# A cross-attention layer in one queue order: hundreds of single steps of a hand-placed schedule moved

## The reference

```python
q = hidden_state @ Wq + bq            # 512 x 1024, 32 heads
k = encoder_hidden_state @ Wk + bk    # 512 x 256, 8 heads
v = encoder_hidden_state @ Wv + bv
scores = jnp.einsum('bkgld,bksd->bkgls', q, k) * scale + mask
attn = jax.nn.softmax(scores, axis=-1)
out = jnp.einsum('bkgls,bksd->bkgld', attn, v)
out = out.transpose(0, 3, 1, 2, 4).reshape(b, l, H) @ Wo + bo
x = out + hidden_state
return (x - mu) * jax.lax.rsqrt(var + EPS) * gamma + beta
```

## Time and profile before

| | us |
|---|---|
| median of 3 runs | 1751.57 |
| lowest and highest | 1750.95, 1754.67 |
| the profiled execution | 1751.32 |
| its span | 1749.3 |
| TensorE matmuls busy | 1602.6 (92%) |
| VectorE busy | 1448.7 (83%) |
| ScalarE busy | 1385.7 (79%) |
| GpSimd busy | 935.7 (53%) |

### The profile page before, as it was taken

One profiled execution on the slowest core, in us unless ns is written; L12 is line 12 of the kernel. 1 busy time (PEld: TensorE's weight loads), 2 busy tenths in 40 slices (PEclk: granted clock), 3 DMA queues, 4 the chain that ended last, 5 costly groups with the idle time before them and its releaser, 6 DMA issues. The chain is left out here.

```text
span 1749.3 us, 38438 instructions
## 1 busy us (share of the span) xinstructions
PE 1602.6 (92%) x14048; PEld 1110.0 (63%) x14048; DVE 1448.7 (83%) x2773; ACT 1385.7 (79%) x3186; POOL 935.7 (53%) x731
## 2 busy tenths in 40 slices
PE   3898879999899989999899998999989999999986
PEld 2665556576566765676576775667666676667654
DVE  4489878789788996889888898789988899788886
ACT  3578868769888787978889789787888878887794
POOL 5426433526754458534675448662585545856382
PEclk8999999999999999999999999999999999999998
DMA  9669987646885578664796567965678646875331
GB/s 178 186 148 227 241 232 199 182 135 168 250 257 144 138 187 286 188 154 122 209 288 185 130 175 192 287 178 127 174 238 252 158 133 170 292 208 150 84 114 67
DMA packets 357292, 325.02 MB, mean 186 GB/s; under 512 B 145776, under 2 KB 248176, under 8 KB 357104
## 3 DMA queue, kind: packets, MB, share of 16 engines
q1 hardware_dynamic: 357104, 322.56, 67.5%
HBM read 244.85 MB, written 83.89 MB: 188 GB/s over the span
## 5 line engine op out<-in xcount | busy, mean ns | idle before, releaser
L1941 PE MATMUL bank<-ring_hi,w_sb 128*128 128x512 f32 x2368 | 785.5, 399 | 32.1 <-issue 19.2
L1725 ACT ACTIVATE probs<-probs,shift 128x512 f32<-128x512 f32 x1024 | 726.9, 713 | 92.1 <-DVE shift L1826 91.0
L1839 DVE STREAM_TRANSPOSE turned_p<-probs 128x2048 f32<-128x2048 f32 x256 | 585.7, 2297 | 154.3 <-PE bank L2021 149.3
L1826 DVE CUSTOM_DVE_ANT_0 probs<-bank,mask_l 128x512 f32<-128x512 f32 x1024 | 643.1, 680 | 56.3 <-PE bank L2001 37.2
L1626 POOL TENSOR_TENSOR w_sb<-w_raw,w_sb 128x512 fp32r<-128x512 f32 x320 | 412.1, 1297 | 413.8 <-ACT w_sb L1682 413.7
L1941 PEld LDWEIGHTS bank<-ring_hi,w_sb 128*128 128x128 f32 x2368 | 444.4, 189 | 149.9 <-issue 42.6
L1941 PE MATMUL bank<-ring_lo,w_sb 128*128 128x512 f32 x1184 | 467.9, 395 | 0.0
L2001 PE MATMUL bank<-k_stack,q_stack 96*128 96x512 f32 x1024 | 358.9, 414 | 12.7 <-DVE shift L1826 10.0
L2021 PE MATMUL bank<-turned_p,v_all 32*32 32x512 f32 x8192 | 307.9, 642 | 65.8 <-DVE turned_p L1839 48.6
L1638 POOL TENSOR_TENSOR ring_lo<-x_t,ring_hi 128x512 fp32r<-128x512 f32 x168 | 214.7, 1291 | 144.9 <-ACT ring_hi L1694 144.4
L2001 PEld LDWEIGHTS bank<-k_stack,q_stack 96*128 96x128 f32 x1024 | 186.1, 189 | 143.3 <-issue 62.9
(11 more groups left out here) (75 smaller groups left out, 933.2 us busy)
## 6 DMA issues: line engine op xcount, KB each, us to landing
w_raw<-w_d SPq DMA_DIRECT2D x144, 256.0 KB, 3.7
q_stack<-q_hi_d SPq DMA_DIRECT2D x128, 256.0 KB, 4.3
w_raw<-in_L_xattn_Wo_dram SPq DMA_DIRECT2D x128, 256.0 KB, 3.0
q_hi_d<-part_hi SPq DMA_DIRECT2D x64, 256.0 KB, 3.9
q_lo_d<-part SPq DMA_DIRECT2D x64, 256.0 KB, 5.0
q_stack<-q_lo_d SPq DMA_DIRECT2D x64, 256.0 KB, 3.9
v_all<-v_d SPq DMA_DIRECT2D x256, 64.0 KB, 2.2
out_dram<-y_sb SPq DMA_DIRECT2D x32, 512.0 KB, 3.0
```

The lines of the kernel that those rows point to most:

```text
L1725: nc.scalar.activation(probs[:, st % 2, h, :], probs[:, st % 2, h, :], ACT.Exp, scale=-1.0, bias=shift[:, g % 2, i:i + 1], accum_out=sums[ ...
L1826: nc.vector.tensor_tensor_reduce(out=probs[:, st % 2, h, :], in0=S_ps[h][:, :], in1=mask_l[:, st, :], scale=-1.0, scalar=HIGHEST, op0=ALU. ...
L1839: nc.vector.transpose(turned_p[:, :, :, st, :].rearrange("p j h c -> p h j c"), probs[:, st % 2, :, :].rearrange("p h (j c) -> p h j c", c ...
L1941: mm = nc.tensor.matmul(C[c][:, :], w_sb[:, n_w, (1, 0, 0)[third], d % 4, :], (hi, lo, hi)[third], start=(n == 0), stop=(n == 23))
```

## The change

BASE and most tables of PLACES get new numbers. No code other than the tables differs, and the steps are the same steps; what differs is the order in which some of them stand in the engines' queues. In the first stage the load of kv 0's second half moves ahead of the input X, the first half of Q 0's weights moves ahead of X's second half, and the tile Q 0 is placed in two parts. Its core, with BASE and the first stage's tables:

```diff
-BASE = {1: 256.32, 2: 463.56, 3: 671.62, 4: 879.00, 5: 1086.39, 6: 1293.78, 7: 1501.17}
+BASE = {1: 254.02, 2: 462.49, 3: 670.73, 4: 878.19, 5: 1085.66, 6: 1293.12, 7: 1500.59}
...
-        "x_load X": (9.8, 15.6),
-        "x_turn X": (22.64, 23.83, 25.27, 26.71, 29.87, 30.51, 32.18, 33.62),
-        "x_hi X": (23.4, 24.65, 26.03, 27.47, 30.63, 31.88, 33.13, 34.38),
-        "x_lo X": (24.47, 25.91, 27.35, 28.22, 31.38, 32.82, 34.26, 35.13),
+        "x_load X": (11.6, 17.4),
+        "x_turn X": (23.67, 24.78, 26.22, 27.66, 30.9, 31.54, 33.21, 34.65),
+        "x_hi X": (24.43, 25.68, 26.99, 28.42, 31.66, 32.91, 34.16, 35.41),
+        "x_lo X": (25.42, 26.86, 28.3, 29.17, 32.41, 33.85, 35.29, 36.16),
...
-            (19.62, 20.09, 20.55, 21.01, 21.47, 21.94, 26.18, 26.65, 27.11, 27.57, 28.03, 28.5),
-            (38.97, 39.43, 39.89, 40.36, 40.82, 41.28, 41.75, 42.21, 42.67, 43.14, 43.6, 44.06),
+            (19.62, 20.09, 20.55, 21.01, 21.47, 21.94, 22.4, 22.86, 23.33, 23.79, 24.78, 25.25),
+            (38, 38.47, 38.93, 39.39, 39.85, 40.32, 40.78, 41.24, 41.71, 42.17, 42.63, 43.1),
...
         "w_load kv": (
-            (8, 13.8),
+            (8, 9.8),
             (23.2, 25),
-            (29.96, 37.19),
-            (39.97, 42.75),
+            (26.8, 32.02),
+            (39, 41.78),
...
-        "keep kv": (29.18, 44.99, 50.3, 55.86),
-        "hi kv": (29.86, 45.67),
-        "lo kv": (30.61, 46.42),
-        "store kv": (33.05, 50.1),
+        "keep kv": (26.31, 44.02, 49.33, 54.89),
+        "hi kv": (27.62, 44.7),
+        "lo kv": (28.37, 45.45),
+        "store kv": (30.66, 49.14),
         "mm Q": (
-            (33.41, 33.88, 34.34, 34.8, 35.26, 35.73, 36.19, 36.65, 37.12, 37.58, 38.04, 38.51),
+            (27.21, 27.78, 28.25, 29.22, 30.09, 30.56, 34.44, 34.9, 35.36, 36.21, 37.08, 37.54),
         ),
         "w_load Q": (
-            (19.6, 21.4),
+            (15.6, 21.4),
         ),
         "w_hi Q": (
-            (31.26, 32.51),
+            (25.06, 32.29),
         ),
         "w_lo Q": (
-            (32, 33.29),
+            (25.8, 33.03),
```

More of the change, by code:

```diff
@@ L136 @@
[L136 to L142, removed]
+            (63.03, 69.44, 74.48, 76.78),
+            (88.56, 94.28, 100.01, 102.31),
+            (109.05, 116.83, 122.56, 125.5),
+            (135.67, 141.35, 149, 151.3),
+            (158.75, 165.16, 172.26, 175.45),
@@ L161 @@
[L161 to L164, removed]
[8 rows of a table removed]
+            (83.52, 84.04, 84.56, 87.15),
+            (109.05, 109.57, 110.09, 110.61),
+            (132.78, 133.3, 133.82, 134.34),
+            (158.58, 159.1, 159.62, 160.14),
+            (183.17, 183.69, 184.21, 184.73),
@@ new lines @@
+            (214.68, 215.2, 215.72, 216.24),
+            (238.84, 239.36, 239.88, 240.4),
+            (258.46, 258.98, 259.5, 260.02),
+        ),
+        "stack": (50.04, 74.23, 83.12, 103.83, 120.16, 142.8, 171.09, 196.28),
+        "recip": (79.08, 107.35, 129.08, 153.6, 174.56, 207.06, 230.49, 256.76),
+        "spread": (79.4, 107.67, 130.6, 154.78, 174.88, 207.88, 231.2, 257.08),
+        "v_load": (61.27, 63.07, 85.82, 109.83, 134.78, 159.36, 183.97, 215.46),
+        "pv": (79.2, 104.73, 127.92, 154.26, 177.87, 210.36, 234.33, 254.14),
@@ L358 @@
-        "o_store": (42.75, 65.28, 97.62, 124.84, 153.15, 181.12, 205.74, 229.83),
-        "mask": (-25.15, -18.33, -8.17, -2.77),
[11 rows of a table removed]
+            (54.1, 54.62, 55.14, 56.29),
+            (84.02, 84.54, 85.06, 85.58),
+            (113.15, 113.67, 114.19, 114.71),
+            (135.3, 135.82, 136.34, 136.86),
+            (163.06, 163.58, 164.1, 164.62),
+            (190.36, 190.88, 191.4, 191.92),
+            (218.14, 218.66, 219.18, 219.7),
+        ),
+        "stack": (-19.57, -5.35, 13.76, 40.05, 62.4, 95.38, 121.94, 147.62),
@@ L399 @@
+            (139.41, 146.16),
+            (150.15, 158.51),
+        ),
[4 rows of a table added]
         "mm q": (
@@ L515 @@
-        "y_add o": (68.88, 74.67, 97, 100.24, 102.22, 122.47, 128.44, 147.58),
+            (38.07, 46.07),
+            (48.78, 54.89),
+            (60.31, 69.34),
+            (74.64, 77.22),
+            (78.51, 82.75),
+            (86.85, 95.54),
+            (101.69, 107.19),
+            (111.27, 113.27),
+        ),
+        "keep o": (66.87, 73.22, 78.9, 92.74, 100.27, 107.78, 124.53, 129.35),
+        "v_turn": (None, None, 159.5, 183.85),
+        "v_store": (None, None, 161.23, 185.85),
@@ L525 @@
-        "z_store o": (171.78, 182.02, 192.52, 200),
-        "root o": 152.47,
-        "rstd o": 162.54,
+            (101.43, 102.08, 103.61, 105.63),
+            (147.52, 148.37, 149.02, 150.56),
+        ),
+        "res o": (-75.28, -74.83, -74.38, -73.93),
+        "aggr o": (148.17, 150.36, 151.21, 152.1),
+        "z o": (165.83, 167.68, 172.77, 181.34),
+        "zmul o": (167.11, 174.59, 183.36, 195.33),
+        "zadd o": (169.56, 179.62, 190.3, 197.78),
+        "z_store o": (173.01, 183.07, 193.75, 201.23),
@@ L528 @@
+        "root o": 152.48,
+        "rstd o": 163.13,
     },
@@ new lines @@
+            (161.37, 161.89, 163.04, 163.56),
+            (187.91, 188.43, 188.95, 189.47),
+            (216.97, 217.49, 218.01, 218.53),
+        ),
+        "stack": (-13.22, 1.69, 18.3, 38.92, 63.16, 94.77, 120.28, 142.04),
+        "recip": (27.5, 51.82, 70.94, 110.86, 131.81, 160.23, 183.55, 203.12),
+        "spread": (27.82, 52.14, 71.26, 111.18, 132.13, 162.06, 184.27, 209.91),
+        "v_load": (-19.31, 11.56, 30.38, 54.3, 83.64, 111.76, 133.01, 161.88),
+        "pv": (25.28, 49.2, 77.58, 106.66, 127.91, 156.78, 182.99, 212.53),
```

890 lines of the change are left out of this document (425 added, 465 removed), and 308 rows, old and new, of the table PLACES.

## The result

The kernel after takes 1757.18 us (median of 19 runs, 1753.8 to 1760.36); the kernel before, run beside it, takes 1751.14 (19 runs). The ratio is 1.0031 [1.0022, 1.0039]: slower, by more than the 0.2% that I had called measurable. The profiled execution of after took 1758.63 us, 7.3 more than the 1751.32 of before, and its span is 1756.6 us.

A forecast was written before the change was run, and what follows sets the result against it. TensorE was taken to bound the middle, with room only in the head. 1751.32 - 0.77 (places) + 1.47 (head) = 1752.0 us; own range 1750.0 to 1754.5, for 8 in 10 1747.3 to 1756.7.

The forecast's parts named there:

- What bounds it: Whole kernel: TensorE holds the middle with small gaps, busy 1602.6 of 1749.3 us; only the head has room.
- busy time is nothing lost or gained: Whole kernel: no instruction is added, removed or resized, only queues are reordered, so busy time changes by nothing.
- The head: Up to the first score: last bias column holds keep kv 0 at 32.48; +0.5 us where the places say -0.97.
- the tail: Head, VectorE's x_lo X4 to x_lo X7 ahead of kv 1: 3.1 us later than before, ending at 43.9.
- Rival C: Head: the biases are not felt and the places are right, ending at 1750.6 us; chance 0.15.
- the places: Whole kernel: start times the code's tables give each step; the new ones end 0.77 us sooner.
- The first batches: Batches t = 0 and 1, re-sorted most: the places' net of -0.1 us, no price for the order.
- The middle batches: t = 2 to 6: about +0.1 us each, at most 0.5; third batch's first score to the end +0.3.
- the end of +1.7 per batch: Middle batches t = 2 to 6: upper bound on the price of the new order, +1.7 us per batch.
- Rival B: PV of group 6, t = 2 to 6: one more half-clock stretch, 1.7 us per batch, 1755.4 to 1760.5; chance 0.24.
- Rival A: Fourth batch: its 4.3 us loss, tied to half-clock stretches, doesn't come; 1747.7 or 1746.2 us; chance 0.19.
- The range: Whole kernel: 8 in 10 between 1747.3 and 1756.7 us.

The follow-up runs named there:

- h1: The kernel after with its four bias DMAs issued from ScalarE's queue at the start instead of SyncE's behind the fourth weight load; 1751.48 us, ratio 1.0003 to before.
- e1: The kernel before with the new tables of the first stage and of batches 0 and 1 only; 1752.39 us, ratio 1.0003.
- m2: The kernel before with new places only from place 86 on (groups 3 to 7) in the table of t = 2 to 6; 1749.28 us, ratio 0.9994.
- m1: The kernel before with new places only below place 86 in the table of t = 2 to 6; 1757.96 us, ratio 1.0043.
- e2: The kernel before with the new tables of t = 2 to 7 only; 1757.02 us, ratio 1.0031.
- g4: The kernel after with 3 filler matmuls before PV of group 1 and 8 before PV of group 6, t = 2 to 6; 1750.71 us, 0.9999 of before.
- g3: The kernel before with 3 filler matmuls before PV of group 1 and 8 before PV of group 6, t = 2 to 6; 1746.16 us, ratio 0.9976.
- g1: The kernel after with 3 filler matmuls before PV of group 1 alone, t = 2 to 6; 1762.55 us, ratio 1.0066 to before.

## What was right in the prediction and what failed, point by point

The forecast was 1752.0 us and, at 0.57, no difference that can be told; the kernel takes 1757.18 and the difference can be told. The direction was right and the size was not.

**What bounds it.** Right as to TensorE and to the head. I had read the middle as "small gaps", though the earlier trace rows also say that a part of its busy time is matmuls at half clock. That part moved most, and with it fell the premise "busy time is nothing lost or gained": the same matmuls keep TensorE busy for 8.6 us longer.

**The head: right in place and mechanism.** Keep kv 0 stayed at 32.48 as forecast, and the wait was 7.30 us (near 7 forecast). Of the chain, x_lo X2 was forecast from 33.85 and ran at 33.72, X3 was done at 36.11 (36.2), w_hi of the second half of Q 0 ran at 37.30 (37.3), and the tail ended at 43.22 (43.9). kv 1 started at 44.08 (44.6), so the term was +0.03 at the first score instead of +0.5. The count of loads was off, without harm: 28 stand ahead of the fourth weight load and 32 ahead of the bias columns, not 24, and in both kernels. Rival C, the places being right there, is refuted by the row, and h1 shows what held them: 5.3 us of gain waited behind those four small DMAs. By an estimate from the fixed cost near 2.0 us that the Trainium skill fits for another issuing path ("DMA: Bandwidth & Descriptors", section "Anatomy of one DMA") the wait would have ended at 31.1; the trace has 32.24 once more.

**The first batches: inside the bounds.** I took -0.1. The third batch's first score came +1.4 late in the profile of after and +0.9 in that of e1, and e1's ratio of 1.0003 can't tell that from nothing.

**The middle batches: the step that failed.** "The sum from the third batch's first score to the end is +0.3 by the places" was the term that was mis-sized. It measured +5.5 in the middle and +0.4 behind it. Two things were missing in it. First, the places did not see a direct cost: they give +0.08 us per batch where like batches show +0.3 to +0.45 at t = 5 and 6 and about 1 at t = 2. My reason for trusting them, that batches keep to their places within 1 us, bounds the error at 1 us a batch and not at 0.1, and five batches of such an error are larger than the measurable bound. I had written the end of +1.7 per batch, and 5.5 lies in it, but took +0.1 per batch. Second, half clock in a place that I didn't look at.

**Rival B: right in kind, wrong in place.** It had a chance of 0.24, a price of 1.7 us per stretch, and 1755.4 to 1760.5 us; 1757.18 lies there, in part by luck, since more of the loss goes with the order than with half clock (below). I placed it at PV of group 6, where the standstill shrank as I had argued (3.21 to 2.81), and m2 shows that those moves cost nothing. The added stretches stand at PV of group 1, a standstill of 1.7 us that I had passed over because the clock had never fallen there in the one profile I had. Each cost 1.5 to 1.6 us in PV itself (4.46 to 5.96 or 6.06). The Trainium skill, "TensorE: Matmul & The Clock Gate", section "What's actually happening", says that the instant of looking isn't tied to the program. m1's two like standstills, one with the fall and one without, agree with it, and on the new order the fall is met in 9 of 20 batches. I had let that widen the range and move no term.

**Rival A** didn't come: t = 3 takes 211.3 where it took 211.7. Its mechanism was wrong, too. Of the stretches that it named, the one at 658.0 to 661.5 lies in the third batch, not the fourth; the fourth did have two, of 3.4 us each. After, it has one, m2's has one, and they still take 211.3 and 210.6: what sets this batch apart is idle time of TensorE, 12.0 us before and 13.0 after, where the others have 9 to 10. **The range** ended at 1756.7, 0.5 us under the median.

**What stays open.** How the 5 to 6 us divide. In the profile of after nearly all of it is busy time (+6.1 busy, -0.6 idle). In m1, with nearly the same total of 1048.1, it is 2.1 busy and 3.3 idle, and in e2, with 1048.2, it is 3.5 busy and 2.0 idle. The repeated runs say more than one profile each. Within those of before beside e1 and e2 a thousandth of clock goes with 1.06 us. At that price (my estimate) the mean granted clock, 0.9712 in after against 0.9736 in those runs of before, accounts for 2.5 of 6.0 us; 0.9730 in e2 for 0.6 of 6.1; 0.9720 in m1, against 0.9746 in the before beside it, for 2.8 of 6.8; and 0.9764 in g4 against 0.9778 in g3 for 1.5 of 4.6. What is left, 3.1 to 5.5 us, goes with the order and not with the clock. So both parts are real, the order's own is the larger, and I can't give either better than within 2 us. Which single moved step of the early part brings it wasn't tried.

## What to carry to other kernels

A planner's places tell what an order means to do, and one unmodelled wait ahead of a chain makes all of them void: look for the operand that is issued last and used first, and move it before moving anything else (5.3 us here, against nothing measurable for the whole re-sorted head). Where an order repeats, an error of half a microsecond a batch is most of the result, so bound the sum over the batches and not one batch. Price every short standstill of the bounding engine, not only the longest: here the clock fell at one of 1.7 us in every other batch. And compare the mean granted clock over repeated runs before a loss is put down to it; the one profile of after shows more of the clock than its runs do. Standstills that can't be removed may be worth filling with idle matmuls, all of them and no longer than the gap; filled too long they cost 14 to 21 us, and with one of two filled the kernel was 5 us slower, for a reason not found.

## What the runs showed of the hardware that I had not expected

- The granted clock fell to half after standstills of 1.72 to 1.73 us that had solid work before them (9.70 of 9.70 us in 1140.0 to 1149.7 of after), in some batches and not in others of the same order; in 20 batches with 1.61 to 1.70 us it never did.
- With one of two standstills filled the fall at the other was longer (6.8 and 10.2 us, g1), but the half-clock time of the five batches the same as unfilled (34.1 us). With both filled the half-clock time of the whole profile was 74.5 us (g3) against 90.8 (before).
- One and the same program spreads by its clock: over 23 executions of before, spans go from 1745.0 us at a mean clock of 0.977 to 1754.9 at 0.969, with a correlation of -0.95. In two other groups of 24 and 23 it is -0.86 and -0.84.
- Four small DMAs, the bias columns, issued from a queue behind 32 loads, held up the first score by 5.3 us. They took that queue 4.3 us to issue (24.72 to 29.00); from ScalarE's queue at the start they took 2.1 us (0.73 to 2.88), and the first load was then waited for until 9.57 us instead of 8.80.
